# Self attentions on one Trainium2 core: value products of two slots divided by key tile, those over the first 128 keys one slot sooner

## The reference

```python
scores = jnp.einsum('bhtd,bhsd->bhts', q, k) * scale      # + mask, or + bias
attn = jax.nn.softmax(scores, axis=-1)
out = jnp.einsum('bhts,bhsd->bthd', attn, v)
```

## Time and profile before

| | |
|---|---|
| median of three runs | 4342.0 us |
| span of the profiled execution | 4397.2 us |
| TensorE busy | 3437.7 us (78%) |
| VectorE busy | 2793.4 us (64%) |
| ScalarE busy | 2088.0 us (47%) |
| GpSimd busy | 1182.3 us (27%) |
| value products, TensorE (line 1468) | 449.8 us busy, 7168 instructions |
| mean granted TensorE clock | 0.867 of full |

### The profile page before, as it was taken

The page is one execution under the profiler, slowest core; times in us unless marked ns, Lnnn a source line. Parts: engine busy times, 40 slices in busy tenths (PEclk is TensorE's granted clock), DMA queues, the critical chain, the costliest instruction groups (busy, mean ns, idle before and its releaser), DMA issues. The chain is left out here.

```text
span 4397.2 us, 86721 instructions
## 1 busy us (share of the span) xinstructions
PE 3437.7 (78%) x30670; PEld 2240.3 (51%) x30670; DVE 2793.4 (64%) x7633; ACT 2088.0 (47%) x4656; POOL 1182.3 (27%) x2276
## 2 busy tenths in 40 slices
PE   6886888896888658759998989677993588869882
PEld 2443554463555338734454545343553466669882
DVE  5884675264786575547676777476865468954453
ACT  2664665232443435426666766443660234335551
POOL 2322221011111234540101110133322422234555
PEclk9987998797998679969999999787995599879996
DMA  5323331033221322230202021223322230122322
GB/s 89 64 35 55 56 56 22 15 95 49 32 39 14 57 70 67 76 58 21 42 24 38 25 38 27 37 53 54 55 35 65 80 92 19 59 70 85 91 80 62
DMA packets 320664, 231.40 MB, mean 53 GB/s; under 512 B 45491, under 2 KB 305168, under 8 KB 320188
## 3 DMA queue, kind: packets, MB, share of 16 engines
q1 hardware_dynamic: 306444, 198.57, 22.8%
q0 software_dynamic: 12928, 26.50, 2.1%
q10 hardware_dynamic: 864, 0.79, 0.1%
HBM read 68.43 MB, written 55.53 MB: 28 GB/s over the span
## 5 line engine op out<-in xcount | busy, mean ns | idle before, releaser
L1373 ACT ACTIVATE PT<-ps 128x512 f32<-128x512 f32 (+1 forms) x1600 | 812.2, 559 | 468.7 <-PE ps L1433 223.0
L1323 DVE TENSOR_REDUCE M<-ps 128x2 f32<-128x512 f32 x1024 | 655.3, 684 | 236.1 <-PE ps L1307 209.3
L1286 PE MATMUL ps<-SKB 49*128 49x256 bf16 (+2 forms) x3584 | 422.6, 275 | 131.7 <-DVE M L1323 53.5
L1320 DVE TENSOR_REDUCE M<-ps 128x3 f32<-128x384 f32 x768 | 390.6, 550 | 180.5 <-PE ps L1304 119.5
L1468 PE MATMUL ps<-PT,VA 128*9 128x256 f32 (+1 forms) x7168 | 449.8, 370 | 1.3 <-ACT PT L1373 1.0
L3847 ACT ACTIVATE SKB<-ps,SKB 128x128 f32<-128x128 f32 x1032 | 295.5, 372 | 279.6 <-PE ps L3765 194.6
L1413 PE MATMUL ps<-SKB 51*128 51x256 bf16 (+2 forms) x3584 | 362.6, 267 | 59.4 <-DMA SKB<-MT 37.0
L3911 DVE COPY SKB<-SKB 128x1028 f32 (+1 forms) x258 | 186.6, 723 | 287.0 <-PE ps L3774 167.7
L1286 PEld LDWEIGHTS ps<-SKB 48*128 48x128 bf16 (+1 forms) x3584 | 137.8, 95 | 427.9 <-issue 131.0
L3774 PE MATMUL ps<-SKB 128*128 128x128 f32 x2064 | 288.7, 285 | 29.9 <-ACT SKB L3847 22.1
L3765 PE MATMUL ps<-SKB 128*128 128x128 f32 x2064 | 293.4, 288 | 0.0
(11 more groups left out here) (497 smaller groups left out, 6720.8 us busy)
## 6 DMA issues: line engine op xcount, KB each, us to landing
SKB<-HH SPq DMA_DIRECT2D x1212, 64.0 KB
SKB<-HH SPq DMA_DIRECT2D x576, 32.0 KB
PT<-L_sorted_rows SPq DMA_DIRECT2D x258, 64.0 KB
L_sorted_results<-SKB SPq DMA_DIRECT2D x258, 64.0 KB
SKB<-in_L3f_w SPq DMA_DIRECT2D x32, 256.0 KB
L_sorted_rows<-TV SPq DMA_DIRECT2D x2, 4032.0 KB, 29.4
SKB<-scratch SPq DMA_DIRECT2D x2, 2048.0 KB, 11.0
SKB<-in_L1f_w SPq DMA_DIRECT2D x16, 256.0 KB
```

The source lines that it names most:

```text
L1286: k = e.matmul(self.mx_bank(m + i)[:, o:o + n], K.QS[self.set(c)][64 * i:64 * i + rows, s, 256 * bb + 128 * qt:256 * bb + 128 * qt + 128], ...
L1320: k = e.tensor_reduce(K.M3[n % 2][:, hh, 0:3], mx[:, 0:384].rearrange("p (a k) -> p a k", a=3), axis=AX.X, op=ALU.max)
L1323: k = e.tensor_reduce(K.M3[n % 2][:, hh, 0:2], mx.rearrange("p (a k) -> p a k", a=2), axis=AX.X, op=ALU.max)
L1373: e.activation(K.PT[:, x % 4, n * i:n * i + n], self.st_bank(x, i)[:, 0:n], ACT.Exp, bias=0.0, scale=self.scale).then_inc(*self.exp.inc())
```

## The change

`pe_pv` takes the key tile `kt` as an argument and issues one half of the group: four products. The half over keys 0 to 127 (`kt` = 0) is issued in slot LE + 2j + 2, with all three waits. The half over keys 128 to 255 (`kt` = 1) stays in slot LE + 2j + 3, with no wait of its own, and its last product increments `pv`. Nothing else is changed.

```diff
-    def pe_pv(self, e, u, j):
+    def pe_pv(self, e, u, j, kt):
...
-        if j % 2 == 0 and f > 0:
+        if kt == 0 and j % 2 == 0 and f > 0:
             e.wait_ge(*self.tv.at(f - 1))
-        if j == 0 and bb == 0 and self.units[u][1] == 0:
+        if kt == 0 and j == 0 and bb == 0 and self.units[u][1] == 0:
             e.wait_ge(*(self.vact if self.W["vb"] is None else self.vdve).at(c))
-        e.wait_ge(*self.exp_done(x + 1))
+        if kt == 0:
+            e.wait_ge(*self.exp_done(x + 1))
         g = j % 2
-        for kt in range(2):
-            for i in range(4):
...
+        lo = 128 if kt == 1 and self.causal else 0
+        o = 256 if kt == 1 else 0
+        for i in range(4):
...
-        k.then_inc(*self.pv.inc())
+        if kt == 1:
+            k.then_inc(*self.pv.inc())
...
         for j in range(4):
-            u = self.at(g, LE + 2 * j + 3)
-            if u is not None:
-                self.pe_pv(e, u, j)
+            for kt in range(2):
+                u = self.at(g, LE + 2 * j + 2 + kt)
+                if u is not None:
+                    self.pe_pv(e, u, j, kt)
```

More of the change, by code:

```diff
@@ L1456, in pe_pv @@
         x = self.nx * u + 2 * j
-        if j % 2 == 0 and f > 0:
+        if kt == 0 and j % 2 == 0 and f > 0:
             e.wait_ge(*self.tv.at(f - 1))
-        if j == 0 and bb == 0 and self.units[u][1] == 0:
+        if kt == 0 and j == 0 and bb == 0 and self.units[u][1] == 0:
             e.wait_ge(*(self.vact if self.W["vb"] is None else self.vdve).at(c))
-        e.wait_ge(*self.exp_done(x + 1))
+        if kt == 0:
+            e.wait_ge(*self.exp_done(x + 1))
         g = j % 2
-        for kt in range(2):
-            for i in range(4):
[L1465 to L1470, removed]
-        k.then_inc(*self.pv.inc())
+        lo = 128 if kt == 1 and self.causal else 0
+        o = 256 if kt == 1 else 0
+        for i in range(4):
+            pt = K.PT[:, (x + i // 2) % 4, 0:2 * self.width].rearrange("p (a k) -> p a k", a=2)
+            k = e.matmul(K.PS[32 * i:32 * i + 9, 6, 256 * g + lo:256 * g + 256],
+                         K.VA[self.set(c)][:, (2 * bb + kt) * 16 + 8 * (i % 2) + 2 * j + i // 2, :], pt[:, i % 2, o:o + 256 - lo],
+                         start=kt == 0, stop=kt == 1)
+        if kt == 1:
+            k.then_inc(*self.pv.inc())
     def pe_gate(self, e, u):
```

## The result

The changed kernel takes 4369.0 us (median of four runs, 4363.22 to 4375.37), the kernel before 4342.2: a ratio of 1.0071 (95% interval 1.0051 to 1.0091), 27 us slower by the medians and 31 by the ratio. The forecast was 4320, faster.

A forecast was written before the change was run, and what follows sets the result against it. No engine alone bounds the kernel: light slots are set by a loop through the vector engine, heavy ones by TensorE's queue. Terms -31 - 5 + 8 + 6 = -22 us took the median 4342 to 4320, range 4292 to 4362.

The forecast's parts named there:

- the loop of 1.61 us: "Add" stage slots without value products: set by a loop through the vector engine, a maximum freeing a bank for the next products.
- The cut: Splitting each value-product group repeats 0.12 us of going in and out of that form: 54 us more TensorE time at full clock.
- Pair B: Value slot followed by a light slot without TV transposes, twice a unit: 3.68 us becomes 3.26 in the "add" stage, saving 0.42.
- Pair A: Value slot followed by a slot with TV transposes, twice a unit: costs 0.10 us in the "add" stage, waiting for ScalarE's copy.
- The "add" stage: Fourth self attention, 48 of 112 units: 0.64 us saved per unit, -31 us in all.
- the unevenness: "Add" stage: other work falling in some light slots leaves less room; a fifth of the gain taken off, +6 us.
- The three other kinds: Causal, unmasked and bias self attentions, 64 units: zero, zero and -5 us, with bounds of -19 to +19 us together.
- Half clock: Self attentions, 194 us with TensorE at half clock: nothing hides and the extra price of splitting doubles, +8 us.
- No change: Rival, chance 0.28: light slots have no room after all, 0.53 us of cover against 0.55 of work; 4340 us.
- clock gained: Rival, chance 0.05: more even work keeps a quarter of 194 us at full TensorE clock, another 24 us; 4295 us.
- The TV copy: Rival, chance 0.14: first halves wait behind ScalarE's copy of TV, 0.42 us each cancelling the gain; 4370 us.
- Full drain: Rival, chance 0.03: the array empties at each switch of product form, 0.31 us a group instead of 0.12; 4375 us.

The follow-up runs named there:

- bare cuts: Against the kernel before, only odd head groups whose light slot holds no other planner TensorE work are cut and moved one slot earlier, 125 cuts: 0.9979.
- occupied ones: Against the kernel before, only odd head groups whose light slot holds other planner TensorE work are cut and moved one slot earlier, 99 cuts: 1.0089, 4379.0 us.
- forced alone: Against the kernel before, all groups cut but both halves stay in the old slot, apart only where mask products stand between (384 groups): 1.0133, 4455.2 us against 4394.7.

## Why the prediction was wrong, point by point

- *What bounds the kernel, and the loop of 1.61 us.* Right for the slots seen: 1.64 after.
- *Half a group, 0.55 us.* Right as measured from the first product's start. *The cut, 0.12*: mis-sized; 0.22, since 0.10 lies ahead of the first value product. Where TensorE waits for the vector engine in that slot anyway the wait covers it; elsewhere it is paid.
- *Pair B saves 0.42, twice a unit.* Half right: 0.40 for slots 0 and 1, 0.03 for 4 and 5. I read one pair in the timeline and took the other for the same. The one not read has the negation of the maxima and their turn (L657) in it. Worth 48 x 0.39 = 19 us of the -31.
- *Pair A costs 0.10, twice a unit.* 0.06 and 0.22: near, 4 us in 48 units.
- *The "add" stage, -31 (with the unevenness, -25).* Measured -5.5 in the kernel with this stage alone. With group 3 alone, half of the 19 us saved went to the chain between repetitions and half to the TV copy in slot 2. Neither was in the sum.
- *The three other kinds, -5 with bounds of -19 and +19.* **This is the step that failed.** Measured +30 to +36, outside the bounds. The costing asked how much cover the vector engine leaves and never listed what else is queued in the light slots of those stages: I took the picture of the "add" stage, where they are bare in 41 of 48 units (slot 4), to stages where every second or nearly every one is occupied. The experiment with bare and occupied slots shows this; a line of the timeline of each stage would have. In the last causal stage, at full clock in both traces, it can be read term by term: the two pairs A cost 7 us in 16 units where their 0.2 each gave 6, and the two pairs B, which were to save as much, cost 3. In the bias stage the cover wasn't there: TensorE is idle for 63 us of it before and 62 after, by the windows, while its busy time grows from 310 to 326 us. The new waits of value products (17.7 us) only take the place of others.
- *Half clock, +8.* In sign right, and too small in one stage: causal + cross has a mean clock of 0.92 where it had 0.96. Twice what is missing to 1 is 58 us at the lower level instead of 27, and half of the 31 more, some 15 us, is time lost. The unmasked, bias and "add" stages keep 0.91, 0.91 and 0.97. What makes the clock fall more often there isn't shown, and a part may be scatter: in the kernel with bare cuts it is 0.94, with occupied ones 0.93, but also 0.94 (and the stretch 346.6) in the kernel with the edit in the "add" stage alone, which is unchanged there.
- *The sum, -22.* Measured +27 to +31. The two terms that were mis-sized, 19 for the "add" stage and 30 + 5 or more for the other stages (which has the clock of causal + cross in it), turn -22 into +32; the smaller ones stay within the spread.
- *Rivals.* No change and clock gained: no. The TV copy (4370) gives the number, but not by its mechanism: 14.3 us in 29 waits (the weight loads alone: 38.6 us in 106), where it asked for 0.42 in each of 224; without the wait more than half of the loss is still there. Full drain (4375): the direction is right, a cut costs more than 0.12, but 0.22 and not 0.31, and it counts only where TensorE's queue is the limit. The real rival, "the light slot is occupied", was absent, though it was a case in which the change ends on the other side with a sharp condition.

The range (4292 to 4362) missed by 7 us, for the bounds of the unread stages were set by half the gain of the read one and not by the full price of a half group in a full slot: 92 occupied slots x 0.3 = 28 us, past the 19 allowed.

The lowest ratios are those of odd groups cut in the "add" stage, or in bare slots only: 0.9978 and 0.9979, some 9 us faster than before. The intervals reach into that of the "add" stage cut whole (0.9989), so the order of the three isn't shown.

## What to carry to other kernels

Before work is moved into a "light" slot, list what stands in that slot in every stage and every unit, the planner's occasional projections and turns too; a slot that is light in the longest stage may be full in the others, and there, unless the engine waits anyway, moved work costs its whole price plus that of the cut. Price a cut from the last foreign product ahead of it to the first behind it, not from its own first start. In a loop over repetitions, look at the chain from a repetition's output to the next one's input: it takes back a part of what faster slots save.

## What the runs showed of the hardware

Going into and out of the four-strip form costs 0.22 us a time (0.10 ahead, 0.12 behind) where it was forced alone; as a mean over 384 cuts 0.16. An output projection that follows value products takes 0.10 us longer in the rows shown (1.09 against 0.99 from its start to the next maxima's product).

In these profiles the chips differ outside the self attentions only. The profile of before has 4397.2 - 2069.1 = 2328 us there, that of after 4373.6 - 2108.8 = 2265, and a kernel that is the same there (odd groups of the "add" stage, on the slower chip: 4383.4 - 2061.4 = 2322) goes with the chip. 17 to 19 of these us lie between the bias and the "add" stage and about 40 behind the last causal stage. What in these parts takes longer wasn't looked into. A forecast made against one profiled span can be carried to the median as a difference, as was done, but the two spans may not be subtracted.
